# A graph network in one kernel: each of the gather groups 1 to 4 of a propagation step waits for the group in front of it

## The reference, cut to what matters

```
...
def step(xk, _):
    msg = norm[:, None] * xk[src]
    agg = jax.ops.segment_sum(msg, dst, num_segments=n_nodes)
    return ((1.0 - ALPHA) * agg + ALPHA * h, None)
xK, _ = jax.lax.scan(step, x, None, length=K)        # K = 10, ALPHA = 0.1
...
return jax.nn.relu(out)
```

## Time and profile before

| | us |
|---|---|
| median of 3 runs | 4962.28 |
| lowest and highest run | 4955.96, 4968.58 |
| span of the profiled execution | 6157.9 |
| in it: TensorE busy | 4502.8 (73%) |
| GpSimd busy | 3237.6 (53%) |
| VectorE busy | 2553.7 (41%) |

### The profile page before, as it was taken

One profiled execution on the slowest core, in us unless ns is written; L12 is line 12 of the kernel. 1 busy time (PEld: TensorE's weight loads), 2 busy tenths in 40 slices (PEclk: granted clock), 3 DMA queues, 4 the chain that ended last, 5 costly groups with the idle time before them and its releaser, 6 DMA issues.

```text
span 6157.9 us, 72323 instructions
## 1 busy us (share of the span) xinstructions
PE 4502.8 (73%) x25760; PEld 2814.8 (46%) x25760; DVE 2553.7 (41%) x8838; ACT 1022.9 (17%) x2922; POOL 3237.6 (53%) x3390
## 2 busy tenths in 40 slices
PE   3778477888775445446555788988888898888888
PEld 2556355566554334344444343434443444444344
DVE  6778444445443445555567422222222222222222
ACT  4656311111111000001222200000000000000001
POOL 3232365566555555555553365565656556565655
PEclk8888688899887666667767999989999999999999
DMA  5222222122222222222221555555555555555554
GB/s 136 77 83 79 77 56 52 51 58 59 55 55 57 67 70 75 68 68 69 65 71 42 160 173 159 171 158 164 172 167 164 166 178 166 161 174 161 165 170 135
DMA packets 455501, 686.46 MB, mean 111 GB/s; under 512 B 91793, under 2 KB 237879, under 8 KB 455120
## 3 DMA queue, kind: packets, MB, share of 16 engines
q1 hardware_dynamic: 341188, 454.71, 23.5%
q0 software_dynamic: 107584, 223.83, 14.0%
q10 hardware_dynamic: 6364, 3.20, 0.2%
HBM read 599.50 MB, written 82.31 MB: 111 GB/s over the span
## 4 chain that ended last, share of the span: by engine, by line
PE 42%; another core or an unknown queue 24%; DVE 18%; issue 11%; ACT 3%; DMA 1%; ACTq 0%; SPq 0%; DVEq 0%; POOL 0%; POOLq 0%
PE ps L2007 27%; PE ps L1751 5%; DVE E L2458 4%; DVE B L2538 2%; PE pt L2102 2%; DVE arena L2580 1%; PE ps L1828 1%; PE ps L2093 1%; PE pt L2038 1%; PE ps L2022 1%; DVE O L3023 1%; PE pt L1719 1%; ACT E L1561 1%; DVE scores L3019 1%
## 5 line engine op out<-in xcount | busy, mean ns | idle before, releaser
L2007 PE MATMUL ps<-arena,E 128*128 128x512 fp8e4 (+1 forms) x4900 | 1147.0, 385 | 93.6 <-issue 84.8
L2007 PE MATMUL ps<-arena,A 128*128 128x512 fp8e4 (+1 forms) x4900 | 1142.1, 385 | 62.4 <-issue 60.1
L1052 POOL DMA_INDIRECT arena<-table,src_i x810 | 776.9, 959 | 685.7 <-DMA table<-E 255.0
L1017 POOL DMA_INDIRECT E<-gat_table,src_i x782 | 759.3, 971 | 634.6 <-DVE arena L2580 367.7
L1052 POOL DMA_INDIRECT arena<-x_spill,src_i x810 | 775.3, 957 | 579.0 <-issue 225.8
L1002 POOL DMA_INDIRECT arena<-table,src_i x782 | 742.8, 950 | 583.5 <-issue 217.1
L1751 PE MATMUL ps<-E,arena 128*128 128x352 f32 (+22 forms) x2932 | 783.6, 421 | 241.1 <-DVE E L2458 155.4
L2007 PEld LDWEIGHTS ps<-arena,E 128*128 128x128 f16 x4900 | 471.4, 100 | 648.6 <-issue 193.9
L2007 PEld LDWEIGHTS ps<-arena,A 128*128 128x128 f16 x4900 | 472.9, 100 | 608.9 <-issue 154.8
L1751 PEld LDWEIGHTS ps<-E,arena 128*128 128x128 f32 x2932 | 515.4, 211 | 441.4 <-issue 195.5
L2909 DVE SCALAR_TENSOR_TENSOR C<-ps,sc_b,scores 128x128 f32<-128x128 f32 x490 | 138.9, 345 | 1295.1 <-PE ps L2022 769.3
(11 more groups left out here) (350 smaller groups left out, 4557.6 us busy)
## 6 DMA issues: line engine op xcount, KB each, us to landing
arena<-adj SPq DMA_DIRECT2D x180, 1024.0 KB
arena<-adj SPq DMA_DIRECT2D x90, 1088.0 KB
adj<-E SPq DMA_DIRECT2D x39, 784.0 KB
arena<-table,src_i POOLq DMA_INDIRECT x1592
O<-dst_rows SPq DMA_DIRECT2D x112, 224.0 KB
arena<-adj SPq DMA_DIRECT2D x20, 768.0 KB
x_spill<-A SPq DMA_DIRECT2D x55, 256.0 KB
arena<-x_spill,src_i POOLq DMA_INDIRECT x810
```

Source lines behind the costliest of these rows:

```text
L1017: pool.indirect_dma_start(out=att_rows[:, b % 3 * AB + at, :], out_offset=None, in_=gat_table, in_offset=bass.IndirectOffsetOnAxis(ap=src_ ...
L1052: pool.indirect_dma_start(out=y_rows[:, g % ERING, k, :], out_offset=None, in_=(table, x_spill)[half], in_offset=bass.IndirectOffsetOnAxis ...
L2007: mm = pe.matmul(chunk_banks[n % 2][:, 0:len(some) * P], y[:, i, h * D:(h + 1) * D], adj_ring[:, piece % ADJ_RING, 0:len(some), at:at + P] ...
```

## The change

On GpSimd, as a step begins, each of the groups 1 to 4 is issued only when all gathers of the group in front have landed. The wait is on the semaphore of that group's slot: what it held before this step, plus 16 for each gather of the group. Group 0 and the groups from 5 on are issued as before. It is four waits a step and 40 in all; the data, the transfers and every other engine's instructions stay as they are.

```diff
@@ -1046,6 +1046,9 @@
                             settle(pool)
                             for g in range(EGROUPS):
                                 pool.wait_ge(sem("edge_used"), pairs * (2 * EGROUPS) + (half * EGROUPS + g + 1))
+                                if 1 <= g < ERING:
+                                    pool.wait_ge(y_in[g - 1], (2 * pairs + half) * row_loads[g - 1] + y_in_before[g - 1]
+                                                 + 16 * group_size(g - 1))
                                 settle(pool)
                                 for k in range(group_size(g)):
                                     tile = edge_first + g * EG + k
```

## The result

The changed kernel takes 5065.61 us, median of 4 runs (5056.82 to 5077.24); the kernel before takes 4965.43 beside it (4 runs, 4955.96 to 4978.32). The ratio is 1.0204, with a 95% interval of 1.0175 to 1.0232: slower by about 101 us. That is above the predicted 4990, above the forecast's own 4970 to 5010, and above the whole range, which ended at 5025.

The account below looks back on a forecast made before the run. TensorE and GpSimd's gathers were taken to keep almost the same pace in layer 3, the gathers' lead deciding. Losses of 5.5 + 7.8 + 8.0 + 7 = 28 us on 4962 gave 4990 us, range 4948 to 5025.

Parts of the forecast that it names:

- The order of work, the pace and the period: Layer 3: TensorE works in fixed order, 220.6 us a step; gathers 5.0 us a group, 7.0 when held.
- Steps 3 to 9: Layer 3's last seven steps: a lead of 9.9 us hides the holds; 0 to 2.6 us lost each, 1 taken.
- the landing: From the start of a group's last gather until landed: 3.2 us, taken from group 0.
- the drift: Steps 3 to 9, the 36 groups behind group 4: GpSimd loses 0.12 us on each, 4.3 us.
- Steps 0 to 2: Layer 3's first three steps, with little or no lead: losses of 5.5, 7.8 and 8.0 us.
- The rival of the clock: TensorE's clock falls in the 12 new waits of steps 0 to 2: 20 us more, 5010 us; chance 0.13.
- The rival of hidden waits: Faster gathers or TensorE pauses enlarge the leads: 12 us in all, 4974 us; chance 0.25.
- The rival of the burst: Unbroken gathers at step starts stop TensorE and the change breaks them: 4915 us; chance 0.2.
- the 500 us of excess: Layer 3 in the first profile: 2707 us against 2206 for ten steps; at least 175 the profile's own.
- The signs: Profile after: held groups' first gathers 7.0 us apart; TensorE waits about 2 us in steps 0 to 2, hardly later.

Follow-up runs that it names:

- held_late: The changed kernel with groups 1 to 4 held back in steps 3 to 9 alone; ratio 1.0128 against the kernel before.
- before_again: The kernel before, unchanged, profiled a second time; ratio 1.002, span 4960.8 us, where its first profile spanned 6157.9.
- held_one: The changed kernel with only group 1 held for group 0, in every step; ratio 1.004 against the kernel before.
- noadj_held: The changed kernel without the adjacency loads of steps 3 to 9; 5020.8 us, ratio 1.0152, 63.8 us over the kernel before with the same loads left out.
- light_held: The changed kernel with groups 5 to 39 gathering three tiles instead of four; 4970.74 us, ratio 1.0073, 54.6 us over `light_free`.
- light_free: The kernel before with groups 5 to 39 gathering three tiles instead of four, no holds; 4916.14 us, ratio 0.9963.
- held_early: The changed kernel with groups 1 to 4 held back in steps 0 to 2 alone; ratio 1.0046 against the kernel before.
- after: The profiled execution of the changed kernel, all four holds in every step; span 5056.0 us, runs 5065.61 us.
- held_two_back: The changed kernel with groups 2 to 5 each waiting for the group two in front instead; ratio 1.0007 against the kernel before.
- held_eight: The changed kernel with groups 1 to 8 held back instead of 1 to 4, in all steps; ratio 1.0419 against the kernel before.

## Why the prediction was wrong, point by point

**The order of work, the pace and the period** were right. A step without waits was put at 220.6 us and is 220.4. The period of a held group was put at 7.0; in steps 3 to 9 it is 6.9 to 7.2 for three of the four and 7.5 to 8.2 for one, 28.5 to 29.4 in all for 28.0.

**Steps 3 to 9 failed.** The step of the working that failed is: "At group 4 it is 9.9 + 4 x 4.95 - 28.0 = 1.7 us, no wait. Over the 36 further groups GpSimd loses 0.12 us on each ..., 4.3 us; today 9.9 - 4.8 remains and nothing waits. So these steps lose between 0 and 2.6 us each ... I take 1 us each, 7 us". The step loses 9.2 each, 63 by `held_late`. Three terms of it were mis-sized, the first the most.

First, the landing. The lead was counted against 3.2 us from the start of the last gather, read at group 0 and taken for every group. At group 39 it is 5.7 once the gathers fall behind an adjacency load. Second, the drift, which the sum had at 0.12 a group, is larger: the lead after issue falls from 12.1 at group 0 to 11.1 at group 4, 8.8 at group 20 and 5.2 at group 39, 0.17 a group behind group 4. A group's gathers take 5.03 us on average there and TensorE 4.87, as its last chunk has the shorter products of 384 columns. Third, TensorE reaches group 4 in 19.0 us (4.52, 4.95, 4.54, 4.96) and not in 4 x 4.95. With these terms and the period as measured the sum is 9.9 + 19.0 - 28.6 - 35 x 0.17 - (5.7 - 3.2) = -8.1 us, most of the 9.2. And the 1 us was taken below the bound of 2.6 since pauses of TensorE were to give the lead back; steps 3 to 6 of `before_again` have none.

What decides is the least spare lead in the step. At group 39 the lead is 5.2 to 5.3 in steps 3 to 6, and the changed kernel's waits there end 4.6 to 5.8 us after the issue, 5.0 on average: 0.3 us. GpSimd's 8.9 us at group 4 (mean of steps 3 to 8) less 0.3 is 8.6 of the 9.2.

The same subtraction gives the other kernels, from the leads of `before_again` and what each profile shows of need:

| | late by | spare at its tightest group | so | measured, a step |
|---|---|---|---|---|
| `held_one` | 2.1 | 0.3 (group 39) | 1.8 | 2.1 |
| the change | 8.9 | 0.3 (group 39) | 8.6 | 9.2 |
| `noadj_held` | 8.4 | 5.2 - 1.6 = 3.6 (group 39) | 4.8 | 5.2 |
| `light_held` | 8.8 | 12.3 - 4.9 = 7.4 (group 5, lead of `light_free`) | 1.4 | 1.4 |

The table holds means of steps 3 to 8 and was worked out with the results known; the needs in it are those of the held kernels, which the unchanged kernel's trace doesn't give, as its group 39 lands in 1.5 us. The 0.6 us that the change's row lacks is GpSimd's lateness, which has grown to 9.5 on average by group 39.

The waits themselves are less than the loss, since each costs 0.16 to 0.17 us beside itself: at group 39 TensorE's rows stand 5.84 us apart (3656.37 to 3662.21) for 4.55 (3616.12 to 3620.67), 1.29 more for a wait of 1.12, as the last product's end no longer overlaps. It is the same for the 31 waits of steps 3, 4, 5 and 8 that can be compared so. For the 52 waits that after has more than `before_again` that is 9 us.

**Steps 0 to 2** were put at 21.3 us. `held_early` has 23 (6 to 40), its profile 36 and that of after 33.6 (13.0, 6.9 and 13.7). The leads there are as small as said, and in step 0 smaller: `before_again` waits 0.9 us for its group 0. TensorE waits 9.4 to 9.8 us a step at groups 1 to 4 of the changed kernel. The size was off for the period, 6.9 to 9.9 us for the 7.0 taken, and for the clock.

**The rival of the clock** is partly true, and small. Step 1 of after, GpSimd's holds ahead of groups 1 and 2, then TensorE's groups 0 to 3:

```profile
2985.68 0.94 POOL L1055 DMA_INDIRECT arena<-x_spill,src_i  x1 [3.62 <-issue]
...
2993.64 0.94 POOL L1055 DMA_INDIRECT arena<-x_spill,src_i  x1 [3.27 <-issue]
```

```profile
2984.97 0.36 PE L2041 MATMUL pt<-rows,arena 128*128 128x2 f16 x8 [1.77 <-DMA arena<-x_spill,src_i]
...
2992.93 0.49 PE L2041 MATMUL pt<-rel_i,arena 128*128 128x34 f16 x8 [3.27 <-DMA arena<-x_spill,src_i]
2993.23 6.20 PE L2010 MATMUL ps<-arena,A 128*128 128x512 fp8e4 x22
2999.87 0.39 PE L2041 MATMUL pt<-weight_e,arena 128*128 128x60 f16 x8 [0.44 <-DMA arena<-x_spill,src_i]
3000.10 4.91 PE L2010 MATMUL ps<-arena,A 128*128 128x512 fp8e4 x22
3006.98 0.38 PE L2041 MATMUL pt<-rows,arena 128*128 128x54 f16 x8 [1.97 <-DMA arena<-x_spill,src_i]
3007.20 4.48 PE L2010 MATMUL ps<-arena,A 128*128 128x512 fp8e4 x20
```

Behind the wait of 3.27 us 22 products take 6.20 us instead of 4.91; behind the one of 1.97 nothing is lost. The length of a wait alone doesn't settle it: of the waits of after that are longer than 1.5 us, those of 2.14 us (step 7), 2.39, 2.56 and 2.59 are followed by a stretch at the lower clock, and those of 2.14 (step 8), 2.48, 3.02 and 3.50 aren't. A slow stretch also hides part of the next hold (0.44 us of wait at group 2). By the clock records of the two profiles TensorE spends 39.3 us of layer 3 at the lower clock, for 14.7 in `before_again`. At half speed that is 24.6 / 2 = 12 us of the 95. The Trainium skill ("TensorE: Matmul & The Clock Gate", "HAM oscillation — how this bites in real kernels") warns of this; the rows agree for some of the longer waits, and it isn't where most of the time went. 71.6 us are the waits themselves, 9 what they cost beside that, and 12 the clock: 93 of the 95.

**The rival of hidden waits** is refuted by `held_one` already. It needed gathers faster than 1.25 us or pauses of TensorE, and has neither.

**The rival of the burst** is refuted by `before_again` and by the change: there is nothing to give back. The prediction said that at least 175 of the 500 us of excess were the profile's own. All of it was: `before_again` has 493 us less from group 0 of step 0 to the end. Why that one execution had its pauses stays open; in the eleven profiled since (the changed kernel's and ten more) they didn't come again, so nothing could be tried on them.

**The signs.** Gathers 7 us apart, and waits at groups 1 to 4 of steps 0 to 2: both there. "Hardly" any waits in steps 3 to 9: wrong, 5 to 8 us each.

Of the kernels tried here that do all of the work none beats the kernel before. The nearest is `held_two_back`, which can't be told from it.

## What to carry to other kernels

Where a producer and a consumer keep nearly the same pace (5.0 and 4.9 us a group here), lost lead isn't won back. A delay at the start of a step shows up thirty groups later, and has to be set against the spare lead of the tightest group, not of the first. Take the landing time from that group's rows too, and ask what the delay puts ahead of it: group 39 landed 1.5 us after its gathers with an adjacency load issued 0.3 us behind them, and 4.7 with the load issued 1.4 us ahead of their end.

Waiting for the item in front turns a stream into a chain in which each link pays its landing; waiting for the one two in front cost nothing clear of the noise.

And a profile that spans a quarter more than the runs should be taken again before any of its pauses is given a cause.

## What the runs showed of the hardware

GpSimd goes on 0.76 to 0.78 us after the last update of the semaphore that it waits for, in all 40 holds of the changed kernel and in those of `held_one`, `held_late`, `held_eight`, `light_held` and `noadj_held`; 0.30 of it stand ahead of every gather. TensorE's waits in after end 0.05 us behind the same kind of update.

The least period of a group of four under a hold is 6.9 to 7.0 us, with adjacency loads or without. It comes out as 3.75 to the start of the last gather, 0.94 for it, 1.5 to its landing and 0.76. Longer ones are the third of steps 3 to 9 (7.5 to 8.2, and 7.8 to 8.0 in four of these steps of `noadj_held` too) and those of steps 0 to 2, up to 9.9.

Gathers almost alone on the DMA engines landed in a median of 1.56 us after their issue had ended (`noadj_held`), next to the adjacency's loads in 2.66 (`before_again`), and at worst there in 6.4.
